# Graph-network tail: the stores of the sums issued by ScalarE on its own queue instead of by SyncE

## The reference

```python
def hconv(x, W, b, node_idx, edge_idx, hw):
    x = x @ W.T
    D = segment_sum(hw[edge_idx], node_idx); Dinv = where(D > 0, 1 / D, 0)
    Bdeg = segment_sum(1, edge_idx);         Binv = where(Bdeg > 0, 1 / Bdeg, 0)
    e = segment_sum(Binv[edge_idx] * x[node_idx], edge_idx)
    return segment_sum(Dinv[node_idx] * e[edge_idx], node_idx) + b
h = hconv(x, W1, b1, ...)
h = gamma * (h - h.mean(0)) * rsqrt(h.var(0) + eps) + beta
x = layernorm(x + hconv(h, W2, b2, ...))
```

## Time and profile before

| | |
|---|---|
| median of three executions | 2722.7 us |
| profiled execution, its time | 2724.19 us |
| its span, first to last instruction | 2722.4 us |
| around the span | 1.8 us |
| POOL busy | 1996.4 us, 73% |
| DVE busy | 1665.9 us, 61% |
| PE busy | 1454.9 us, 53% |
| ACT busy | 880.2 us, 32% |
| mean granted TensorE clock | 0.77 |

### The profile page before, as it was taken

The page is one execution under the profiler, slowest core; times in us unless marked ns, Lnnn a source line. Parts: engine busy times, 40 slices in busy tenths (PEclk is TensorE's granted clock), DMA queues, the critical chain, the costliest instruction groups (busy, mean ns, idle before and its releaser), DMA issues. The chain is left out here.

```text
span 2722.4 us, 22417 instructions
## 1 busy us (share of the span) xinstructions
PE 1454.9 (53%) x4577; PEld 733.9 (27%) x4577; DVE 1665.9 (61%) x5028; ACT 880.2 (32%) x1963; POOL 1996.4 (73%) x1591
## 2 busy tenths in 40 slices
PE   6676548888727556536777826634554661012111
PEld 1233224444413222212333314412222331001110
DVE  8999837878836777684778744423433555434443
ACT  0111115766724565561565621201111321000000
POOL 5777767777538888855577777778874786777777
PEclk9999869999957787767898968868777885555555
DMA  1111124444244555524355446757786784323331
GB/s 25 17 28 28 20 74 116 128 126 116 80 100 114 112 123 125 127 63 100 98 122 124 110 94 197 202 144 180 186 146 194 216 221 112 92 60 72 72 75 43
DMA packets 353928, 298.10 MB, mean 109 GB/s; under 512 B 106729, under 2 KB 308224, under 8 KB 353777
## 3 DMA queue, kind: packets, MB, share of 16 engines
q1 hardware_dynamic: 252993, 225.49, 29.9%
q0 software_dynamic: 100800, 71.18, 14.7%
HBM read 199.79 MB, written 96.90 MB: 109 GB/s over the span
## 5 line engine op out<-in xcount | busy, mean ns | idle before, releaser
L2024 PE MATMUL tl_pX<-k_ident,tl_ga 125*128 125x125 f32 x400 | 85.2, 351 | 446.5 <-DMA tl_ga<-table_TE,k_s_idxE 337.5
L2135 DVE TENSOR_TENSOR_SCAN tl_S<-tl_same,tl_S,tl_pX 128x500 f32<-128x500 bf16 x96 | 120.3, 1253 | 316.0 <-issue 166.2
L439 POOL DMA_INDIRECT tl_ga<-table_TE,k_s_idxE x200 | 244.2, 1221 | 63.5 <-issue 58.9
L439 POOL DMA_INDIRECT eq_ga<-table_T,k_idxS x100 | 125.7, 1257 | 81.9 <-ACT eq_y L1729 52.8
L2024 PEld LDWEIGHTS tl_pX<-k_ident,tl_ga 125*128 125x128 f32 x400 | 57.6, 179 | 462.8 <-DMA tl_ga<-table_TE,k_s_idxE 347.7
L439 POOL DMA_INDIRECT ms_ga<-table_T,k_idxS x100 | 142.4, 1424 | 36.4 <-issue 30.2
L439 POOL DMA_INDIRECT tl_ga<-table_TH,k_send x100 | 123.9, 1239 | 56.7 <-issue 55.8
L1333 POOL DMA_INDIRECT k_pay<-table_ptab,k_clip x100 | 144.5, 1445 | 27.4 <-issue 27.1
L1218 PE MATMUL tl_pCon<-dr_BC,dn_cT 128*128 128x512 f32 x196 | 134.8, 777 | 50.7 <-ACT dn_cT L1225 27.1
L439 POOL DMA_INDIRECT at_ga<-x,at_srcI x100 | 128.5, 1285 | 43.3 <-issue 25.2
L439 POOL DMA_INDIRECT at_gb<-x,at_dstI x100 | 128.0, 1280 | 36.8 <-issue 27.7
(11 more groups left out here) (432 smaller groups left out, 4643.8 us busy)
## 6 DMA issues: line engine op xcount, KB each, us to landing
dr_x<-x SPq DMA_DIRECT2D x97, 256.0 KB
result<-dr_o SPq DMA_DIRECT2D x97, 256.0 KB
dm_xT<-xT SPq DMA_DIRECT2D x32, 768.0 KB
table_T<-at_y SPq DMA_DIRECT2D x50, 250.0 KB
table_T<-ms_y SPq DMA_DIRECT2D x50, 250.0 KB
table_T<-eq_y SPq DMA_DIRECT2D x50, 250.0 KB
table_TE<-tl_y SPq DMA_DIRECT2D x50, 250.0 KB
tl_fac<-table_dinv SPq DMA_DIRECT2D x50, 250.0 KB
```

The lines of the kernel that those rows point to most:

```text
L439: nc.gpsimd.indirect_dma_start(out=buf[:, k, :], out_offset=None, in_=table, in_offset=bass.IndirectOffsetOnAxis(ap=index[:, CT * c + k:CT ...
L2024: last = nc.tensor.transpose(pX[j % 2][:, k * TP:(k + 1) * TP], ga[j % RG][:, k, :], K["ident"][0:TP, 0:TP])
L2135: nc.vector.tensor_tensor_scan(S[i][:], same[j % RM][:], pX[i][:, 0:CE], 0.0 if j % NC == 0 else S[1 - i][:, CE - 1:CE], ALU.mult, ALU.add ...
```

## The change: what it does

`store(j)` leaves SyncE's block and stands in ScalarE's. SyncE's turn no longer has it. ScalarE calls it right behind `out(j)`, in the same turn as before; it waits for its own copy to be complete and then starts the same transfer, from the same buffer to the same place and with the same semaphore, on ScalarE's queue. There are 75 such stores (50 to TE and TE2, 25 to TH).

```diff
@@ block.sync
-            def store(j):
-                sp.wait_ge(s_y, j + 1)
-                sp.dma_start(rows_of(T[TARGET[j // NC]], CE * (j % NC), CT), y[j % 2][:]).then_inc(s_st[j % 2], 16)
-
...
                     load_target_rows(t + 2 - T_NORM)
-                if 0 <= t - 1 < J_LAST:
-                    store(t - 1)
                 if t < J_LAST:
@@ block.scalar
+            def store(j):
+                act.wait_ge(s_y, j + 1)
+                act.dma_start(rows_of(T[TARGET[j // NC]], CE * (j % NC), CT), y[j % 2][:]).then_inc(s_st[j % 2], 16)
+
...
             for t in range(T_END + 2):
                 if 0 <= t - 1 < J_LAST:
                     out(t - 1)
+                    store(t - 1)
                 if norm_turn(t - 1) is not None:
```

## The result

The changed kernel takes 2733.17 us (median of 17 runs, 2723.67 to 2748.4) beside 2721.71 us before (17 runs, 2717.24 to 2731.5). The ratio is 1.0043, 95% interval 1.0026 to 1.0059: slower by 11.5 us, where 9.7 us less than 2722.7 were forecast. 2733 lies outside the range of 2697 to 2729. The profiled execution took 2740.16 us with a span of 2738.3.

The account below looks back on a forecast made before the run. POOL's list of indirect DMAs was taken to bound the kernel, with gains only in two idle gaps. Savings of 4.7 and 6.2 us, 10.9 in all, off 2724.2 us gave 2713 us, range 2697 to 2729 (8 in 10).

Parts of the forecast that it names:

- What bounds: Tail: POOL works through its list of indirect DMAs at 1.51 us each; only shortening its first two idle times can pay.
- the two gaps in the tail: POOL idle 26.48 us before pass 2's first gather (gap 1) and 13.99 us before the first scatter (gap 2).
- SyncE's lag and handover: At set 97, before the first scatter: 2.9 us of lag saved, and 3.2 of the 4.36 us handing over.
- ScalarE's price: 75 store issues on ScalarE at 0.374 us plus waits for its copy, about 35 us; 0.4 us charged before the first scatter.
- Landing: Last store of pass 1, before pass 2's first gather: lands 0.9 us sooner on its own queue.
- The bound of -2 us: Lower bound on the landing gain of pass 1's last store, if it shares with a following dense load.
- Gap 1's "near nothing" for a full DMA: Late pass 1: dense loads arriving sooner without stores in their queue, bounds 0 and 23.4 us, taken as 1 us.
- Gap 2's "upstream, of bounds 0 and 5.61 us I take 0.5": Pass 2, before the first scatter: copy 71's 5.61 us wait, put down to store 69, shortens by 0.5 us.
- The sum: 4.7 us before pass 2 plus 6.2 us before the first scatter: 10.9 us off 2724.2, giving 2713 us.
- The cap on gap 2's gain: The idle time before the first scatter can shrink by about 9.4 us before chunk 3 or store 74 is late.
- Rival 3: ScalarE held at issue, 4.5 us a store, in two turns before set 97: 2730 us; chance 0.13.
- rival 1: Only issue time is saved, since the backlog is the DMA engines' own: 5.3 us off, 2719 us; chance 0.17.

Follow-up runs that it names:

- sp_actwait: Kernel before, stores still on SyncE, with ScalarE waiting for its own copy and running one tiny activation in place of the issue: 2728.75 us, ratio 1.0006.
- act_pass2: Changed kernel with only pass 2's 25 stores on ScalarE's queue, those of passes 0 and 1 from SyncE as before: 2737.49 us, ratio 1.0035.
- act_ring4: Changed kernel with four `y` buffers and four semaphores in place of two: 2731.97 us, ratio 1.0030.

## Why the prediction was wrong, step by step

- *What bounds.* Right: POOL's list and the two gaps in the tail; behind the first scatter nothing moved.
- *SyncE's lag and handover.* Right: 2.9 us and 4.36 us at set 97 became 0.03 and 0.34. Together they took 6.0 us away between combine and scatter, where 6.1 were forecast. The terms are real and fell on an instruction that was itself 15.9 us late.
- *ScalarE's price.* Right in kind and over-sized: 0.26 us an issue, and no cost that shows in `sp_actwait`. The cost came by the other side of ScalarE, its waits for a free buffer.
- *Landing, "I take +0.9, as its queue is empty but for it".* This step failed. An empty queue is not an empty engine: the engines of a store work for SyncE's queue as well. For store 49 alone the landing was even better than taken (5.1 us from issue to release; SyncE's last dense load had been issued 6.3 us earlier). But I priced one store, the last; those before it set when its copy comes. In pass 1 their drain rose from 5.4 to 8.4 us, and copy 49 came 8.0 us later. The bound of -2 us had been taken for that one store from one following load, and not for every landing that a copy waits on.
- *Gap 1's "near nothing" for a full DMA.* "A full DMA does not become faster by another order" was used for dense loads alone. By order it became slower for the stores, and they, not dense rows, hold the copies: ScalarE's waits +43 us, DVE's waits for dense loads -2.7.
- *Gap 2's "upstream, of bounds 0 and 5.61 us I take 0.5".* The wait of copy 71 for store 69 was seen and bounded at zero below. It should have had a side below zero: this is the term that grew: late landings from store 55 on made the combine of set 97 15.9 us late, through copies, coefficients and PE, and that gave the 9.9 us behind gap 1.
- *The sum.* The terms add up to 10.9 us off the profiled execution; that lies 1.5 us above the median, so 2713 should have read 2712. The cap on gap 2's gain is 9.0 us by its own rows (6.2 and 2.8 to spare at chunk 3), not 9.4. Neither touches the outcome.
- *Rivals.* Rival 3 had the sign and about the size (2730), but its place, a hold at issue, is not where the time went (3.75 us once); the place is one step ahead, at `out`. The rule of rival 1, that spreading over issuers saves only the issuer's time, fell as a bound: the transfers are not indifferent to the queue. It holds the better the more engines a store has.

Open: with the stores gone, SyncE also no longer waits for each copy, and its dense loads are handed over in 0.49 us in the median instead of 1.63. So the dense loads stand beside the stores partly because they come earlier, and no run keeps SyncE's wait while ScalarE issues; how much is the second queue and how much the earlier loads is not separated. The turns on one engine are inferred from drains, since no record names the engine. Which single landings decide differs from run to run (with pass 1 unchanged, copy 44 waits 9.67 us in before and 24.31 in `act_pass2`). Nor is it shown why splitting the target rows gave nothing.

## What to carry over

Before a transfer is moved to another queue, count its packets and its DMA engines, and ask what else those engines carry: here many small packets on few engines drained more slowly beside big ones of another queue (8.4 us for 5.4 in pass 1) than behind them on the same queue. Price the landing of every transfer that hands back a buffer, not only of the last one, and give it a bound on both sides. If rows allow it, first cut the transfer so that it covers all engines (here 112 + 13 for 125 partitions, -0.6%); which engine issues it is then nearly free to choose.

## What was unexpected of the hardware

- An issue on a queue with three or four transfers that may be under way on few engines can be held, up to 25.00 us on ScalarE (`act_ring4`), and the engine's compute instructions with it; with at most two under way an issue is 0.26 us in the median and 3.75 at most.
- A gather's packet of 4 KB takes 1155 ns in the mean in the slow stretch of pass 1 (2000 to 2045 us; 1074 after), against about 275 in the mean of the whole run. The DMA engines are then busy to 1.00 at only 127 GB/s before and to 0.98 at 141 after, whichever queue carries the stores.
- Two stores a few us apart on a queue of their own land unevenly: in pass 1 the first of a pair sooner (6.3 us for 9.2), the second later (14.4 for 12.4) than on the shared queue, with the same mean.
